# A graph layer on one core: GpSimd clears a small block of its own between two gathers of 128 rows

## The reference, cut to what matters

```python
def _cheb_norm(src, dst, n):
    deg = segment_sum(ones, src, num_segments=n)
    dinv = where(deg > 0, rsqrt(maximum(deg, 1.0)), 0.0)
    return -dinv[src] * dinv[dst]

def _cheb_conv(x, src, dst, norm, W0, W1, b):
    tx1 = segment_sum(x[src] * norm[:, None], dst, num_segments=x.shape[0])
    return x @ W0 + tx1 @ W1 + b

h = _cheb_conv(x, src, dst, norm, W1_0, W1_1, b1)
h = _layer_norm(h, gamma, beta)
h = where(h >= 0, h, 0.01 * h)
out = layernorm(x + _cheb_conv(h, src, dst, norm, W2_0, W2_1, b2))
```

## Time and profile before

| | us |
|---|---|
| median of 3 runs | 3442.92 (3438.34 to 3451.11) |
| span of the profiled execution, first to last instruction | 3370.7 |
| PE busy | 2065.1 (61%) |
| DVE busy | 1544.4 (46%) |
| ACT busy | 505.3 (15%) |
| POOL busy | 1700.9 (50%), of it 1672.6 in 1664 gathers |
| gathers' packets, share of the 16 DMA engines' span | 45.9% (the other two data queues 7.2% and 3.6%) |

### The profile page before, as it was taken

The page is one execution under the profiler, slowest core; times in us unless marked ns, Lnnn a source line. Parts: engine busy times, 40 slices in busy tenths (PEclk is TensorE's granted clock), DMA queues, the critical chain, the costliest instruction groups (busy, mean ns, idle before and its releaser), DMA issues.

```text
span 3370.7 us, 41016 instructions
## 1 busy us (share of the span) xinstructions
PE 2065.1 (61%) x7250; PEld 963.6 (29%) x7251; DVE 1544.4 (46%) x3507; ACT 505.3 (15%) x1030; POOL 1700.9 (50%) x1725
## 2 busy tenths in 40 slices
PE   6836576665665665665764656565565656555655
PEld 5712232222222322232331222222222222222222
DVE  6754444444444444544443444444444434444444
ACT  5920111111111211111230000000000000000000
POOL 0156554545555554655526545554545445554543
PEclk6558887887887878887876878787777777878778
DMA  6376565655555555655646555565555555555554
GB/s 215 133 259 181 150 174 155 173 159 160 164 167 168 159 165 157 181 159 167 182 132 200 166 158 171 166 177 155 167 159 164 155 158 165 161 165 162 159 159 122
DMA packets 215109, 559.98 MB, mean 166 GB/s; under 512 B 48100, under 2 KB 49760, under 8 KB 214948
## 3 DMA queue, kind: packets, MB, share of 16 engines
q0 software_dynamic: 133120, 436.31, 45.9%
q10 hardware_dynamic: 44676, 81.73, 7.2%
q1 hardware_dynamic: 37152, 40.21, 3.6%
HBM read 493.08 MB, written 64.18 MB: 165 GB/s over the span
## 4 chain that ended last, share of the span: by engine, by line
PE 30%; another core or an unknown queue 26%; issue 25%; DVE 8%; ACT 5%; DVEq 3%; ACTq 1%; DMA 1%; POOL 1%; SPq 0%; POOLq 0%
PE bank L749 16%; PE bank L710 10%; DVE acc L947 6%; PE bank L668 2%; ACT work L556 2%; ACT feat L564 1%; DVEq L923 1%; PE bank L727 1%; PE bank L655 1%; DVEq L947 1%; DVE onehot L923 1%; POOL ring L444 1%; ACT work L546 1%; ACTq L528 0%
## 5 line engine op out<-in xcount | busy, mean ns | idle before, releaser
L444 POOL DMA_INDIRECT ring<-table,index x1664 | 1672.6, 1005 | 1466.5 <-SPq L393 952.1
L947 DVE SCALAR_TENSOR_TENSOR acc<-bank,down,acc 128x512 f32 x928 | 696.9, 751 | 1219.6 <-PE bank L710 709.8
L710 PE MATMUL bank<-ring,onehot 128*128 x3712 | 920.3, 406 | 306.0 <-issue 148.1
L749 PE MATMUL bank<-wA,feat 128*128 128x512 f32 x784 | 547.6, 863 | 804.2 <-ACT feat L564 748.2
L923 DVE TENSOR_SCALAR onehot<-count_h,dst_c,neg_tile 128x128 f16<-128x128 f16 x1856 | 489.2, 329 | 490.1 <-issue 487.6
L710 PEld LDWEIGHTS bank<-ring,onehot 128*128 128x128 f16 x3712 | 380.6, 103 | 865.6 <-issue 515.3
L749 PEld LDWEIGHTS bank<-wA,feat 128*128 128x128 f32 x784 | 212.0, 285 | 1084.9 <-ACT feat L564 774.3
L727 PE MATMUL bank<-wB,base_in 128*128 128x512 f32 x784 | 353.6, 594 | 0.0
L546 ACT ACTIVATE work<-acc 128x512 f32 (+1 forms) x98 | 61.7, 630 | 1747.4 <-issue 1039.3
L727 PEld LDWEIGHTS bank<-wB,base_in 128*128 128x128 f32 x784 | 149.5, 191 | 155.8 <-issue 142.1
L564 ACT ACTIVATE feat<-bank 128x512 f32<-128x512 f32 x98 | 58.5, 597 | 845.4 <-remote 828.7
(11 more groups left out here) (118 smaller groups left out, 689.6 us busy)
## 6 DMA issues: line engine op xcount, KB each, us to landing
ring<-table,index POOLq DMA_INDIRECT x1664
base_in<-feat ACTq DMA_DIRECT2D x98, 256.0 KB
feat<-feat SPq DMA_DIRECT2D x49, 256.0 KB, 2.9
table<-work SPq DMA_DIRECT2D x49, 256.0 KB, 3.1
feat<-feat ACTq DMA_DIRECT2D x49, 256.0 KB
table<-work ACTq DMA_DIRECT2D x49, 256.0 KB
feat<-in_x ACTq DMA_DIRECT2D x48, 256.0 KB
out<-work ACTq DMA_DIRECT2D x48, 256.0 KB
```

The lines of the kernel that those rows point to most:

```text
L444: nc.gpsimd.indirect_dma_start(out=ring[:, at * ROW:(at + 1) * ROW], out_offset=None, in_=table[l], in_offset=bass.IndirectOffsetOnAxis(ap ...
L710: last = nc.tensor.matmul(bank[u % SUM_BANKS][:, :], onehot[:, u, j, :], ring[:, bass.ds(at, D)], start=j + half == 0, stop=j + half == GROUP)
L749: last = nc.tensor.matmul(to[:, :], feat[:, 2 + tile_slot, c * P:(c + 1) * P], wA[:, c * D:(c + 1) * D], start=False, stop=c == KB - 1)
L947: nc.vector.scalar_tensor_tensor(tile_of(acc, tile[u]), bank[u % SUM_BANKS][:, :], col(down[:, l, :], tile[u]), tile_of(acc, tile[u]), ALU ...
```

## The change

Behind each gather GpSimd now waits for its own clearing of two gathers ago (`paced`), counts `gathers_begun` up, and clears one of the two halves of a new block `pace` (128x128 float32 each), which nobody reads. The groups that TensorE loads, and the steps that SP loads, are now unsigned 16-bit numbers (`group_u`, `used_u`); VectorE makes `group_u` with one more copy.

```diff
+U16 = mybir.dt.uint16
...
+        pace = sb("pace", [P, 2, P], FP32)
...
+        group_u = sb("group_u", [1, WALK], U16)
         slot_i = sb("slot_i", [1, WALK], I32)
-        used_i = sb("used_i", [1, GROUPS], I32)
+        used_u = sb("used_u", [1, GROUPS], U16)
...
+        paced = sem("paced")
...
-                        used_i[0:1, bass.ds(it.n * UNROLL - FREE_LAG + first, UNROLL - first)],
+                        used_u[0:1, bass.ds(it.n * UNROLL - FREE_LAG + first, UNROLL - first)],
...
                                 bounds_check=bound, oob_is_err=False).then_inc(ring_landed[k], 16)
+                            before = (GROUPS * l + it.n * UNROLL + k) * GROUP + j
+                            wait(pool, paced, before - 1 if l or it.least * UNROLL * GROUP + at > 1 else 0)
+                            pool.sem_inc(gathers_begun, 1)
+                            nc.gpsimd.memset(pace[:, at % 2, :], 0.0).then_inc(paced, 1)
...
-                    for t, top in ((group_i, GROUPS - 1), (slot_i, RING - 1)):
+                    for t, top in ((group_u, GROUPS - 1), (slot_i, RING - 1)):
...
+            link(nc.vector.tensor_copy(group_u[:, :], group_i[:, :]))
-            link(nc.vector.scalar_tensor_tensor(used_i[:, :], count[0:1, 0:GROUPS], 1.0, bank[7][0:1, 0:GROUPS],
+            link(nc.vector.scalar_tensor_tensor(used_u[:, :], count[0:1, 0:GROUPS], 1.0, bank[7][0:1, 0:GROUPS],
                                                 ALU.add, ALU.add))
```

## The result

| | us | ratio to before |
|---|---|---|
| before | 3442.92 | |
| after | 3304.93 (3303.02 to 3321.56) | 0.963 [0.959, 0.968] |

About 4% faster, where 3115 (9.5%) was forecast. The profiled execution's own time is 3303.0, its span 3301.2: 1.8 us lie around the span, and about as much in the later runs. So most of the 72.2 carried for that in the prediction was that before's profiled execution was 2% under the median.

The account below looks back on a forecast made before the run. It took a hold on TensorE's semaphore, kept up by trains of gathers, as the bound. Hold gone: 1664 x 1.55 + 359 = 2938 us; a fifth of visits still held: 3116, stated as 3115, range 2850 to 3800.

Parts of the forecast that it names:

- a hold on TensorE's semaphore: ACT's copy L564 sees TensorE's finished turns only 3.0 us after the train's last gather starts; 828.7 us of remote waits.
- The 3829: Total in us if the hold stays: 3443 plus 386 for longer gaps between gathers, all on the path.
- The clearing: +0.25 us a gather: GpSimd's memset behind each gather adds 0.25 us, between 0.14 and 0.35, taking the pitch from 1.30 to 1.55.
- Four of five visits freed: Share of ACT's copy visits expected to lose the hold: 2938 + 0.2 x (3829 - 2938) = 3116 us; break-even 43%.
- What 1.55 would have given: Forecast pitch in us between gather starts on GpSimd; with the hold gone, 1664 x 1.55 + 359 = 2938 us.
- The cost of the held visits: If the hold stays, 13.3 pitches a block lengthen by 0.25 us over 116 blocks: 386 us on the path.
- The new wait: 0: GpSimd's wait for the clearing before last costs 0, as more than a gather's 1.00 us is queued meanwhile.
- Rival C: The clearing's own semaphore is held like TensorE's, so GpSimd stops every two or three gathers: 4190 us; chance 0.04.
- U16: 0: 16-bit list loads on TensorE cost 0, between gaining 0.27 and losing 0.56 us each; one extra VectorE copy, 0.65 us.
- Rival A: The hold is only stretched by the longer pitch, so the kernel gets slower: 3829 us (3659 to 4230); chance 0.32.
- rival B: Hold gone but memset dear: at a pitch of 1.82 GpSimd eats the gain, 3387 us; chance 0.08.
- D: Gain and cost cancel with about 43% of visits freed: 3443 us; with other mixtures near it, chance 0.05.

Follow-up runs that it names:

- e4: Changed kernel with 512 float16 columns cleared behind each gather instead of 128 float32: 3124 us, 0.906 of before.
- e3: Changed kernel with 256 float32 columns cleared behind each gather instead of 128: 2857 us, 0.830 of before.
- e11: Changed kernel without the clearing, 16-bit lists kept, 16 already met waits ahead of each gather: 2446 us, 1.002 of before.
- e9: Changed kernel without the clearing and with 32-bit lists masked in a register: 2443 us, 1.001 of before.
- e1: Changed kernel without the clearing and its wait, only the 16-bit lists left: 3404 us, 0.986 of before.
- set 4: A later set of runs sharing one chip, with the changed kernel rerun unedited; before took 2446 us there.
- e12: The changed kernel itself, unedited, run again in a later set: 2598 us, 1.063 of before.
- e7: Changed kernel without the clearing, 16-bit lists kept, each gather bringing half the bytes in as many rows: 3352 us, 0.993 of before.

## Why the prediction was wrong

The direction and the mechanism held in the set that was measured, the size did not. Two steps failed, one behind the other: the clearing was put too dear, and with the short pitch that came of it only a few visits were freed.

- *The bound is a hold on TensorE's semaphore, kept up by the train of gathers.* Right for the sets with the hold: e4 removes it with a longer pitch and the same order of work, and the "remote" wait goes with it. That the turns are issued and their count comes late is read from starts (the next matmuls follow on them, the copy doesn't); matmul ends in the profile are modelled. The Trainium skill's sentence "PE and ACT never wait on anyone" ("SBUF — State Buffer", "Who interferes with whom") is about SBUF ports. The 3829 that the prediction drew from it is refuted by e3 and e4; the sentence itself, which does not speak of semaphores, is not touched by these runs.
- *The clearing: +0.25 us a gather.* It measured 0.085, below the lower bound of 0.14. The duration was right (0.22 against 0.21), and the start too: 1 ns behind the gather's end at the median, so no part of it lies under the gather. But it was added to the 0.30 us between two gathers, and it takes the place of a part of it: 0.165 stays. The bounds only asked how much of the clearing lies under a gather, not how much of the idle time lies under the clearing. The nearest row for that was in view: L406 and L407 begin 0.14 us apart and last 0.21. By the rule of the Trainium skill ("GPSIMD Engine Reference", "Instruction dispatch") the clearing could have begun under the gather; this trace shows no sign of that, with its start 1 ns behind the gather's end.
- *Four of five visits freed.* This is the step that carries the miss. At 1.389 only 22 of 98 visits are free, where four of five were forecast. The cheaper clearing alone would have moved the forecast away from the result: with 1.389 the hold gone is 1664 x 1.389 + 289 = 2600 and the hold kept 3443 + 131 = 3574 (next point), and four of five freed give 2600 + 0.2 x 974 = 2795. With the measured share the same sum is 2600 + (76/98) x 974 = 3355, 1.5% above the 3305 measured. The share was guessed from trains with one longer pitch, half of which were freed, and held nothing on how much longer the pitches must be. The runs show that this decides: of before's 90 held visits one in six was freed at 1.389 (76 left), and about six in ten at 1.469 and 1.495 (32 and 39 left).
- *What 1.55 would have given* no run shows. Between e3 (1.495) and e4 (1.709) the sum with the hold gone is 2868 there (1664 x 1.55 + 289), and these two came out 80 over and 9 under their sums. So a result near the forecast is likely at the pitch that it assumed, but not by its own mixture: at 1.495 that would give 2777 + (39/98) x (3735 - 2777) = 3158, and 2857 was measured. The held copies of e3 start 3.7 us after the turns at the median, where before has 9.1, so a held visit costs less there than the forecast put it at.
- *The cost of the held visits.* With 0.085, 13.3 x 0.085 x 116 = 131 us come on top if nothing is freed (estimate). The block above shows it, 28.25 - 27.5 = 0.75 us, a part of the 13.3 x 0.085 = 1.1. The gain of 138 is what the freed visits left over after that.
- *The new wait: 0.* Right: "POOL pace L455" stands in the waits with 0.17 us each, the hand-over itself, and the clearings waited 1.0 us in all. Rival C (its semaphore held too) is refuted, at a pitch of 1.389 no less.
- *U16: 0.* Wrong as to its own duration: 1.55 us a load more, past the bound of 0.56, and 104 on SP besides. Without the hold this costs next to nothing (e11 1.002, e9 1.001). With the hold its effect is not told: e1 was 1.4% faster than before, and no run with 32-bit lists met the hold.
- *Rival A* (only stretched, 3829) is refuted by e3 and e4, *rival B* came true only at 512 columns, where the memset is dear, and *D*, both sides cancelling at 3443, was 138 us off, nearer in time than the 190 of the forecast, though it wanted 43% freed. Of the signs named ahead, the "remote" time (697.1, not under 250) and L444's wait for SP (705.6, not under 300) failed, and trains still 14 long would have been read as A. No case asked whether the hold would be there in another run at all, so that the change was faster is in part luck of the set. Without it the same kernel is 6.3% slower than before, which is the side that held 0.37, by a mechanism that was not among the rivals: GpSimd's rate as the bound from the start.

## What to carry to other kernels

When an instruction is put behind another on the same engine, ask what of the existing gap it fills: the cost is the new pitch less the old one, not its duration. Where the chain ends at a releaser that the profile can't name, measure the kernel in more than one set of runs, on other chips if you can, before tuning against it: here the same wait was worth 1000 us in some sets and nothing in others, and the cure cost 6 to 12% where there was nothing to cure. And a cure by spacing must go far enough: a step that stops short pays the spacing and gets little back (0.963 at 1.389, 0.83 at 1.47 to 1.50 us). How much further the best point lies isn't known, as nothing was tried between 1.50 and 1.71, where it is 0.906.

## What the runs showed of the hardware

- With the hold, TensorE's semaphore for finished turns was seen 7 to 10.5 us late (the middle half of the visits in before) while gathers followed at 1.31 us, mostly about 3 us after the last of them began; in after about 2 us. It goes with the rate of gathers (88 of 98 visits at 1.306, 76 at 1.389, 43 at 1.446, 32 at 1.469, none at 1.709), not with their bytes or packets (83 at half and 0.6 of them).
- It is there in some sets only. The changed kernel at the same pitch of 1.389 took 3305 us with 76 visits held, and 2598 with none in set 4; before took 3443 and 2446. What differs, the chip, its surroundings or the hour, is not known.
- Where it is there, the trace has a quarter of the gathers' semaphore increments (6704 of 26624 in before), elsewhere nearly all (26562 in e12). Whether recording takes part in it is not known.
- With it went slow instructions in the queues: register and semaphore instructions of VectorE, SP and TensorE of about 0.7 us, where e12 has 0.02 to 0.2. Over 0.6 us there were 846 in before, 809 in after, 243 at 192 columns, 112 at 256, none at 512 columns, and none in the sets without the hold.
- Eight values of 16 bits took 2.3 to 2.7 us to load on TensorE's queue, eight of 32 bits 0.84 to 0.95 (medians of the group list, after 2.42, e9 0.91).
- An indirect gather of 128 rows kept GpSimd for 1.00 us, of 1 KB (e7) or of 2 KB rows alike.
- A 128x128 float32 clearing began 1 ns behind its gather, lasted 0.22 us, and the next gather began 0.165 later (after, e12), where 0.30 lies between two bare gathers: 0.085 us of pitch.
